# Router, top-2 choice and scatter of a mixture of experts set into local attention's pipeline, and three rounding passes of an FP4 feed-forward set on GpSimd

## Chip, cores and metric

One core of a Trainium2 chip. The metric is device time in microseconds (us) from one launch of the whole program, lower is better. All data are float32.

## What is computed

Four sublayers, one after another, on x of shape (4, 1024, 256). Each adds its output to its input; `_layernorm` has no weights.

```python
x = x + local_attention(_layernorm(x))      # L0_attn: 16 heads, each token sees itself and its two neighbours
x = x + experts(_layernorm(x))              # L0_ffn: 8 experts, top 2
x = x + gated_delta_attention(_layernorm(x))  # L1_attn: a recurrence over 1024 tokens
x = x + fp4_feed_forward(_layernorm(x))     # L1_ffn: 256 -> 704 -> 256

# L0_ffn
logits = x_flat @ router_w + router_b
probs = softmax(logits); top_w, top_idx = top_k(probs, 2)
output = sum over e of comb[:, e] * (gelu(x_flat @ expert_up[e].T) @ expert_down[e].T)

# L1_ffn, before each of its three products
scale = max(|x| in a block of 16) / 6, at least 1e-12
q = nearest of 0, 0.5, 1, 1.5, 2, 3, 4, 6 to |x / scale|, with x's sign, times scale
```

## The kernel before, in words

The program is four blocks in a row, each with its own tiles in memory and its own hand-written instruction streams for the five engines; between blocks all engines meet. Within a block the order on each engine is the order of the calls in its function, and semaphores order the engines against each other. `need(engine, sem, n)` waits until `sem` has reached `n`.

**Local attention** (`local_attention`, L78 to L375). A tile is 128 tokens by 256 features; 32 tiles, taken in 16 pairs, four pairs to a batch row. All engines run through the same steps s = -3 to 17, and in step s each has work on pairs of different age. VectorE: `evict(s)` (queries, keys and values of pair s from PSUM, L230), `scores(s-1)` (L238 to L243), `moments(s+3)` (L203 to L208), `weigh(s-1)` (L248 to L254), `result(s-2)` (L263: projection plus residual). TensorE: `products(s+1, 0)` (L354), `turned_out(s-2)` (L363), `products(s+1, 1)`, `projected(s-2)` (L371), `turned(s+2)` (L343). ScalarE: `turned_out`, `exps`, `normalised(s+3)` (L288) and `turned(s+2)` (L293). GpSimd: `roots(s+3)` (three small instructions, L177 to L179) and `residual(s-1)` (two sums of 256 columns, L184). SyncE loads x, stores results to a stream in device memory, and shifts the keys and values of the edge tiles by one partition for each batch row (L145 to L149), for which `scores` of every fourth pair waits. The first product waits for all loads.

**Mixture of experts** (`mixture_of_experts`, L388 to L787). First the router, over 8 groups of 4 tiles read back from the stream. VectorE: `moments` (L537 to L542), `norm` (normalised rows, L548 and L551), `shift` (bias and maximum of the logits, L555 to L558), `choose` (softmax's sum, the two largest of 8 probabilities, their indices, one-hot counts, L563 to L581), `place` (rank within the expert to row number, L590 to L598). TensorE turns the rows (L704), takes the logits (L713, 16 matmuls) and sums counts (L721, L722). ScalarE copies the turned rows (L660, L665), copies each normalised row for the second expert (L663) and takes the exponentials (L672). GpSimd takes roots (L496) and scatters: for each tile and each of the two choices one indirect DMA of 128 rows into the experts' slots (L491, 64 in all), and at the end 8 more that pad each expert's last tile (L507). ScalarE's DMA queue loads the eight down weights of 1 MB and copies the stream to the accumulator. When the counts are known a table says which expert each of 71 slot tiles belongs to, and where it starts. SyncE waits for all of this and for every scatter, then loads up weights and slot rows tile by tile (L471, L473); TensorE, ScalarE and VectorE work through the 71 tiles, and GpSimd adds the weighted rows into the accumulator (L515).

**Recurrent attention** (`delta_attention`) is not touched by the change.

**FP4 feed-forward** (`fp4_feed_forward`, L1716 on). 32 tiles in 8 trips of 4. `fp4` rounds in nine VectorE passes (L1797 to L1808): block maximum, scale, reciprocal, ratio, exponent bits, a magic number, add it, subtract it, times scale. The hidden rows of each tile (704 columns) are rounded by `round_h`, the normalised rows of a whole trip (1024 columns) at once by `round_z`. VectorE's order per tile n: `result(n-2)` (L1847), `hidden(n)` (two products, L1833), `norm(t+1)` at the second tile of a trip, `round_h(n)`, `round_z(t+1)` behind the third. TensorE: `gate_up(n)` (L1945), `transpose_h(n-1)` (L1955), at the fourth tile `transpose_z(t+1)` (L1934), `down(n-1)` (L1964). GpSimd only takes one root per trip (L1785).

Of the kernel before, what the change touches and what calls it, by code (L numbers as in the profile page):

```python
# [7 lines left out]
ALU = mybir.AluOpType  # L8
# [6 lines left out]
P = 128  # L15
# [62 lines left out]
def local_attention(nc, x_in, consts, w, x_out, B, S, H):  # L78

    DH = D // H
# [4 lines left out]
    scale = DH ** -0.5  # L88
    with ExitStack() as stack:
        m = Scope(nc, stack, "la")  # L90
        ident = m.sb("ident", [P, P]); mhalf = m.sb("mhalf", [P, 1]); neg = m.sb("neg", [P, 2])
        wp = m.sb("wp", [P, KD, D]); wpn = m.sb("wpn", [P, KD, D]); win = m.sb("win", [P, KD, C3]); wc = m.sb("wc", [P, KD, C3]); wo = m.sb("wo", [P, KD, D])
        bp = m.sb("bp", [P, KD]); bpb = m.sb("bpb", [P, KD, P]); braw = m.sb("braw", [P, C3]); bias = m.sb("bias", [P, C3]); bo = m.sb("bo", [P, D])
        x = m.sb("x", [P, 2, TB, D]); z = m.sb("z", [P, 2, 2, D]); zT = m.sb("zT", [P, 2, KD, 2, P])
        st = m.sb("st", [P, 2, 6]); mv = m.sb("mv", [P, 2, 2, 2]); ve = m.sb("ve", [P, 2, 2]); rstd = m.sb("rstd", [P, 2, 2]); nb = m.sb("nb", [P, 2, 2])
        slot = m.sb("slot", [P, 2, TB + 2, C3])
        qk = m.sb("qk", [P, 2, 3, D]); sc = m.sb("sc", [P, 2, 3, H]); mx = m.sb("mx", [P, 2, H]); ex = m.sb("ex", [P, 2, 3, H]); sm = m.sb("sm", [P, 2, H])
        av = m.sb("av", [P, 2, 2, 3, D]); oT = m.sb("oT", [P, 2, KD, 2, P]); xb = m.sb("xb", [P, 2, 2, D]); y = m.sb("y", [P, 2, 2, D])
        ps_qkv = [m.psum(f"ps_qkv{u}", 1024) for u in range(2)]
        ps_z = m.psum("ps_z"); ps_oT = m.psum("ps_oT"); ps_o = [m.psum(f"ps_o{i}") for i in range(2)]  # L100
        loaded = m.sem("loaded"); x_loaded = [m.sem(f"x_loaded{i}") for i in range(4)]; edges = [m.sem(f"edges{i}") for i in range(4)]
        made = m.sem("made"); wpn_psum = m.sem("wpn_psum"); wpn_ready = m.sem("wpn_ready"); wc_psum = m.sem("wc_psum"); wc_ready = m.sem("wc_ready")
# [3 lines left out]
        y_ready = m.sem("y_ready"); stored = [m.sem(f"stored{i}") for i in range(2)]; chain = m.sem("chain"); pool_chain = m.sem("pool_chain")  # L106
        LOADS = 10
        consts["stale"] = m.sems
        in_rows = x_in.rearrange("b (p j) d -> b p j d", j=TB)
        out_rows = x_out.rearrange("(b p j) d -> b p j d", p=P, j=TB)  # L110
        tiles_of = lambda n: [(2 * (n % NP2) + 1 + u) % TB for u in range(2)]
        STEPS = range(-3, NPAIR + 2)
        here = lambda n: 0 <= n < NPAIR
        block = stack.enter_context(nc.Block())
# [6 lines left out]
        def _(sp):  # L121
            def load_x(s):
                b, r = s // NP2, s % NP2
                if s >= 4:
                    need(sp, var_ready, s - 3)
                if s >= 8:
                    need(sp, z_ready, 2 * (s - 7))
                    need(sp, xb_ready, s - 4 if r == 0 else s - 7)
                sp.dma_start(x[:, b % 2, 2 * r:2 * r + 2, :], in_rows[b, :, 2 * r:2 * r + 2, :]).then_inc(x_loaded[s % 4], 16)
# [3 lines left out]
            for dst, src in ((ident[:], consts["ident"]), (mhalf[:], consts["mhalf"]), (wp[:], w["WpT"].rearrange("(k p) n -> p k n", p=P)),  # L133
                             (win[:, :, 0:D], w["WqT"].rearrange("(k p) n -> p k n", p=P)), (win[:, :, D:C3], w["WkvT"].rearrange("(k p) n -> p k n", p=P)),
                             (bp[:], w["bp"]), (braw[:, 0:D], w["bq"].partition_broadcast(P)), (braw[:, D:2 * D], w["bk"].partition_broadcast(P)),
                             (braw[:, 2 * D:C3], w["bv"].partition_broadcast(P)), (bo[:], w["bo"].partition_broadcast(P))):
                sp.dma_start(dst, src).then_inc(loaded, 16)
            sp.dma_start(wo[:], w["WoT"].rearrange("(k p) n -> p k n", p=P)).then_inc(loaded, 16)
# [12 lines left out]
            def store(n):  # L151
                need(sp, y_ready, n + 1)
                for u, j in enumerate(tiles_of(n)):
                    sp.dma_start(out_rows[n // NP2, :, j, :], y[:, n % 2, u, :]).then_inc(stored[n % 2], 16)

            for s in STEPS:
# [4 lines left out]
                if here(s - 3):  # L161
                    store(s - 3)
            store(NPAIR - 1)
            for i in range(2):
                sp.wait_ge(stored[i], 16 * NPAIR)

        @block.gpsimd
        def _(pool):
            pc = Chain(pool, pool_chain)
            pc.link(nc.gpsimd.memset(neg[:], -1.0))  # L170
            pool.wait_ge(loaded, 16 * (LOADS + 1))

            def roots(s):
# [5 lines left out]
                nc.gpsimd.tensor_tensor(nb[:, par, :], nb[:, par, :], neg[:], ALU.mult).then_inc(rstd_ready, 1)  # L179

            def residual(n):
                need(pool, y_ready, n - 1)
                for u, j in enumerate(tiles_of(n)):
                    ins = nc.gpsimd.tensor_tensor(xb[:, n % 2, u, :], x[:, (n // NP2) % 2, j, :], bo[:], ALU.add)  # L184
                ins.then_inc(xb_ready, 1)

            for s in STEPS:
                if here(s + 3):
                    roots(s + 3)
                if here(s - 1):  # L190
                    residual(s - 1)
# [1835 lines left out]
```

## Time and profile before

| | |
|---|---|
| three runs, us | 4022.38, 4025.67, 4015.97 (median 4022.38) |
| the profiled execution, us | 4007.19 |
| its span (first to last instruction), us | 4005.4 |
| mean granted TensorE clock | 0.929 of 2.4 GHz |
| TensorE matmul busy | 3264.1 us, 81% |
| VectorE busy | 2633.9 us, 66% |
| ScalarE busy | 1427.6 us, 36% |
| GpSimd busy | 891.3 us, 22% |

The profile calls the engines PE (TensorE's matmuls), PEld (its weight loads), DVE (VectorE), ACT (ScalarE), POOL (GpSimd) and SP (SyncE); a q behind the name is the engine's DMA queue. L12 is line 12 of the kernel. Tile names begin with their block: la, moe, da, ff. Shares of busy time are means over blocks with different limits, so they are read block by block.

### The profile page before, as it was taken

Reading aid. Unit: us, or ns where it says so; the run is one execution under the profiler, and the core shown is the slowest. Engines: PE = TensorE matmul, PEld = TensorE weight load, DVE = VectorE, ACT = ScalarE, POOL = GpSimd, SP = SyncE. Lnnn points to the kernel's source line nnn. Section 1 sums busy time; section 2 is a strip of 40 time slices with the busy share of each in tenths; the row PEclk is TensorE's granted clock in tenths of the full one; section 3 lists DMA queues with packets and bytes.
Section 4 is the critical chain, followed back from the end, with each engine's and each line's share of the span. In section 5 each row is a group of like instructions: output and inputs, shape, how many; then the busy total and the mean of one; then the engine's idle time right before and its main releaser. Section 6 shows DMA issues by size and latency. Waiting matters only on the chain. (4 is left out here: it accounts for less than half of the span.)

```text
span 4005.4 us, 141798 instructions
## 1 busy us (share of the span) xinstructions
PE 3264.1 (81%) x62854; PEld 2462.9 (61%) x62854; DVE 2633.9 (66%) x5780; ACT 1427.6 (36%) x3252; POOL 891.3 (22%) x1018
## 2 busy tenths in 40 slices
PE   7844999993888888888888888888888888727777
PEld 4633999992566666666655666666566566514555
DVE  6844000002877887887787778877877787667887
ACT  1111212221444454445444444544454444311111
POOL 2316222221223222222322232222223222200000
PEclk9965999996899999999999999999999999858999
DMA  2154666652000000000000000000000000010000
GB/s 63 48 184 143 185 182 179 182 160 89 5 7 11 7 7 11 7 7 7 11 7 7 7 11 7 7 11 7 7 7 11 7 7 5 6 40 14 22 21 14
DMA packets 101423, 172.44 MB, mean 43 GB/s; under 512 B 15128, under 2 KB 75160, under 8 KB 100752
## 3 DMA queue, kind: packets, MB, share of 16 engines
q1 hardware_dynamic: 72592, 127.75, 9.8%
q0 software_dynamic: 19824, 23.03, 4.0%
q10 hardware_dynamic: 8400, 12.58, 0.9%
q8 instruction: 501, 8.21, 0.9%
q14 instruction: 106, 0.87, 0.1%
HBM read 125.35 MB, written 40.05 MB: 41 GB/s over the span
## 5 line engine op out<-in xcount | busy, mean ns | idle before, releaser
L962 POOL TENSOR_TENSOR da_M<-da_M,da_decay 128x512 f32<-128x512 f32 x256 | 279.9, 1122 | 634.8 <-DVE da_M L1125 323.1
L1268 ACT COPY da_Ub<-da_U 32x256 f32<-32x256 f32 x1024 | 412.0, 402 | 17.4
L1102 DVE TENSOR_TENSOR da_eGn<-da_eGn,da_z 128x30 f32<-128x30 f32 (+14 forms) x960 | 352.6, 367 | 33.0
L643 DVE TENSOR_SCALAR moe_y<-moe_ps_dn,moe_zs 128x256 f32<-128x256 f32 x71 | 34.4, 484 | 510.1 <-PE moe_ps_dn L769 510.1
L1101 DVE TENSOR_TENSOR da_z<-da_eGn 128x30 f32<-128x30 f32 (+14 forms) x960 | 348.7, 363 | 27.6
L1554 PE MATMUL da_C<-da_Ub,da_Km 128*64 128x256 f32 x2048 | 302.8, 417 | 23.3 <-ACT da_Ub L1268 9.5
L759 PEld LDWEIGHTS moe_ps_up<-moe_zsT,moe_up 128*128 128x128 f32 x2272 | 266.2, 193 | 5.4 <-ACT moe_zsT L676 1.8
L759 PE MATMUL moe_ps_up<-moe_zsT,moe_up 128*128 128x128 f32 x2272 | 266.9, 276 | 1.2 <-ACT moe_zsT L676 1.2
L1386 PE MATMUL da_unit<-da_wx,da_xnT 128*128 128x512 f32 x512 | 257.8, 628 | 3.7 <-DVE da_sp L1045 2.7
L769 PE MATMUL moe_ps_dn<-moe_down,moe_hT 128*128 x1136 | 256.8, 379 | 0.0
L1393 PE MATMUL da_unit<-da_xnT,da_wx 128*128 128x128 f32 x2048 | 245.5, 279 | 12.4 <-ACT da_eGn L1253 12.4
L1393 PEld LDWEIGHTS da_unit<-da_xnT,da_wx 128*128 128x128 f32 x2048 | 236.8, 194 | 19.9 <-ACT da_eGn L1253 19.9
L1125 DVE TENSOR_TENSOR da_M<-da_C,da_M 128x512 f32<-128x512 f32 x256 | 176.0, 687 | 98.7 <-PE da_C L1554 96.3
L1261 ACT COPY da_U<-da_A 128x256 f32<-128x256 f32 x256 | 95.5, 373 | 379.7 <-PE da_A L1525 378.9
L682 ACT ACTIVATE moe_hT<-moe_ps_up 128x512 f32<-128x512 f32 x142 | 84.8, 597 | 406.2 <-PE moe_ps_up L759 406.2
L769 PEld LDWEIGHTS moe_ps_dn<-moe_down,moe_hT 128*128 128x128 f32 x1136 | 210.5, 190 | 25.6
L1525 PE MATMUL da_A<-da_W,da_TT 32*32 32x64 f32 x8192 | 180.0, 224 | 51.7 <-DVE da_W L1112 30.4
L955 POOL TENSOR_TENSOR da_v<-da_v,da_norm 128x256 f32<-128x256 f32 x128 | 116.7, 1205 | 448.7 <-ACT da_v L1240 448.7
L1554 PEld LDWEIGHTS da_C<-da_Ub,da_Km 128*64 128x64 f32 x2048 | 137.8, 143 | 115.2 <-issue 59.4
L1541 PE MATMUL da_B<-da_U,da_gm 32*32 32x64 f32 x8192 | 171.5, 219 | 42.3 <-ACT da_U L1261 24.5
L1525 PEld LDWEIGHTS da_A<-da_W,da_TT 32*32 32x32 f32 x8192 | 133.9, 109 | 114.1 <-issue 47.9
L515 POOL DMA_INDIRECT moe_acc<-moe_y,moe_zs x71 | 110.0, 1549 | 419.9 <-DVE moe_y L643 417.0
(289 smaller groups left out, 6830.4 us busy)
## 6 DMA issues: line engine op xcount, KB each, us to landing
moe_up<-in_upT SPq DMA_DIRECT2D x71, 1024.0 KB, 5.1
moe_zs<-moe_slots SPq DMA_DIRECT2D x71, 129.0 KB, 4.2
moe_down<-in_downT ACTq DMA_DIRECT2D x8, 1024.0 KB, 12.0
la_x<-in_x SPq DMA_DIRECT2D x16, 256.0 KB, 3.9
stream<-la_y SPq DMA_DIRECT2D x32, 128.0 KB, 2.3
moe_x<-stream SPq DMA_DIRECT2D x8, 512.0 KB, 4.9
da_x<-moe_acc SPq DMA_DIRECT2D x128, 32.0 KB, 2.0
stream<-da_xz SPq DMA_DIRECT2D x128, 32.0 KB, 1.8
```

The source lines that it names most:

```text
L759: ins = nc.tensor.matmul(ps_up[j][:, f * P:(f + 1) * P], up[:, n % UB, k, (j * HB + f) * P:(j * HB + f + 1) * P], zsT[:, n % 2, k, :], sta ...
L769: ins = nc.tensor.matmul(ps_dn[n % 2][:, 0:D], hT[:, n % 2, f, :], down[:, bass.ds(expert[n] + f * D, D)], start=(f == 0), stop=(f == FB - 1))
L962: ins = nc.gpsimd.tensor_tensor(st_, st_, decay[:, par, rec, 2 * g:2 * g + 2].rearrange("p a b -> p (a b)").unsqueeze(2).to_broadcast([P, ...
L1101: c.link(tt(t, Xm[:, s + 1:C, s:s + 1].to_broadcast([P, below, s]), Xm[:, s:s + 1, 0:s].to_broadcast([P, below, s]), ALU.mult))
L1102: c.link(tt(Xm[:, s + 1:C, 0:s], Xm[:, s + 1:C, 0:s], t, ALU.add))
L1125: tt(st_, Cp[:], st_, ALU.add).then_inc((s_updated, r_updated)[rec], 1)
L1268: ins = nc.scalar.copy(Ub[rows_of(b), :, :, b, :], U[rows_of(b), rec])
L1386: ins = mm(bank, xnT[:, par, kk, :], wx[:, kk, u // 2, cols], start=(kk == 0), stop=(kk == KD - 1))
L1393: ins = mm(bank[:, hp * P:(hp + 1) * P], wx[:, kk, j, col:col + P], xnT[:, par, kk, :], start=(kk == 0), stop=(kk == KD - 1))
L1525: ins = mm(wu[rw, q_, 2 + rec, j], TT[rw, of_solve(g, q_, rec, j), :], W[rw, rec, q_, j], start=True, stop=True)
L1541: ins = mm(po[rw, q_, 1, j], gm[rw, par, g, q_, (first + j) * C:(first + 1 + j) * C], U[rw, rec, q_, j], start=False, stop=(rec == 1), ski ...
L1554: ins = mm(Cp[feat(q_), j * B * DH:(j + 1) * B * DH], Km[:, g, rec, j, DH * q_:DH * (q_ + 1)], Ub[:, q_, j].rearrange("p b e -> p (b e)"), ...
```

## The change

`local_attention` now only notes its inputs, and `mixture_of_experts` holds attention, router and experts as one block. The steps run to 22, and `part_of(s, lag)` says which group of four tiles (two pairs), if any, has its router part in step s. A group's moments stand in odd steps, its normalised rows, turned rows, logits and shift in the even step after, exponentials in the next, choice at a lag of 6, places at 7, scatter at 8. Tokens are numbered by attention's own tiles, and results stay in memory for the router while they are stored straight into the accumulator; the read back and the copy are gone. Normalised rows for both choices are made by ScalarE. The residual is added into x's own tile, which has three batch rows of room. Weighted values and projections have one buffer, not two. Down weights lie where the key and value rows were, and are loaded by SyncE behind `av_ready` of the last pair. Padding rows are written by ScalarE's DMA queue at addresses read into a register.

```diff
+            for s in STEPS:
+                if part_of(s, 8) is not None:
+                    scatter(part_of(s, 8))
+                if here(s - 1):
+                    residual(s - 1)
+                if here(s + 3):
+                    roots(s + 3)
+                if part_of(s, 3) is not None:
+                    roots2(part_of(s, 3))
...
+            for s in STEPS:
+                if here(s):
+                    evict(s)
+                if here(s - 1):
+                    scores(s - 1)
+                if s >= 0 and here(s + 3):
+                    moments(s + 3)
+                if part_of(s, 6) is not None:
+                    choose(part_of(s, 6))
+                if here(s - 1):
+                    weigh(s - 1)
+                if here(s - 2):
+                    result(s - 2)
+                if part_of(s, 7) is not None:
+                    place(part_of(s, 7))
+                if part_of(s, 3) is not None:
+                    moments2(part_of(s, 3))
+                if part_of(s, 4) is not None:
+                    shift(part_of(s, 4))
...
+            def router_rows(g, r):
+                b = g % 2
+                need(act, rstd2_ready, g + 1)
+                need(act, scattered[g % XB], (g // XB) * 16 * 2 * ST)
                 for s in range(ST):
+                    nc.scalar.activation(zx[:, g % XB, s, r, 0:D], y[:, b, s, :], ACT.Identity, bias=nb2[:, b, s:s + 1], scale=rstd2[:, b, s:s + 1]).then_inc(z2_ready, 1)
...
+            for s in STEPS:
+                if part_of(s, 4) is not None:
+                    router_rows(part_of(s, 4), 0)
+                if here(s - 2):
+                    turned_out(s - 2)
+                if part_of(s, 5) is not None:
+                    exps2(part_of(s, 5))
+                if here(s - 1):
+                    exps(s - 1)
+                if part_of(s, 4) is not None:
+                    turned_rows(part_of(s, 4), 0)
+                if here(s + 3):
+                    normalised(s + 3)
+                if part_of(s, 4) is not None:
+                    turned_rows(part_of(s, 4), 1)
+                if here(s + 2):
+                    turned(s + 2)
+                if part_of(s, 4) is not None:
+                    router_rows(part_of(s, 4), 1)
...
+            act.wait_ge(pad_ready, 1)
+            for e in range(E):
+                at = act.value_load(padidx[0:1, e:e + 1], min_val=0, max_val=DUMP)
+                act.dma_start(slots[bass.ds(at, P), :], pad[:]).then_inc(padded, 16)
...
+            for s in STEPS:
+                if part_of(s, 7) is not None:
+                    ranks(part_of(s, 7))
+                if here(s + 1):
+                    products(s + 1, 0)
+                if here(s - 2):
+                    turned_out(s - 2)
+                if part_of(s, 4) is not None:
+                    turned_rows(part_of(s, 4), 0)
+                if here(s + 1):
+                    products(s + 1, 1)
+                if here(s - 2):
+                    projected(s - 2)
+                if part_of(s, 4) is not None:
+                    turned_rows(part_of(s, 4), 1)
+                if here(s + 2):
+                    turned(s + 2)
+                if part_of(s, 4) is not None:
+                    logits(part_of(s, 4))
...
+            sp.wait_ge(av_ready, NPAIR)
+            for e in range(E - 1):
+                load_down(e)
             store(NPAIR - 1)
+            load_down(E - 1)
```

In the feed-forward, `round_z` ends on VectorE with the magic number; `norm(t+1)` moves to the first tile of a trip and `round_z(t+1)` behind the second.

```diff
             for t in range(TRIPS):
                 pool.wait_ge(var_ready, t + 1)
                 nc.gpsimd.tensor_tensor(rstd[:], ve[:], mhalf[:].to_broadcast([P, UN]), ALU.pow).then_inc(rstd_ready, 1)
+                pool.wait_ge(z_scaled, t + 1)
+                pc.link(nc.gpsimd.tensor_tensor(zlevel[:], zratio[:], zmagic[:], ALU.add))
+                pc.link(nc.gpsimd.tensor_tensor(zlevel[:], zlevel[:], zmagic[:], ALU.subtract))
+                if t > 0:
+                    pool.wait_ge(zT_psum, t * 2)
+                nc.gpsimd.tensor_tensor(blocks(qz[:].rearrange("p u d -> p (u d)")), blocks(zlevel[:]),
+                                        zscl[:].unsqueeze(2).to_broadcast([P, WIDE // FP4_BLOCK, FP4_BLOCK]), ALU.mult).then_inc(qz_ready, 1)
...
-                if u == 1 and t + 1 < TRIPS:
+                if u == 0 and t + 1 < TRIPS:
                     norm(t + 1)
                 round_h(n)
-                if u == 2 and t + 1 < TRIPS:
+                if u == 1 and t + 1 < TRIPS:
                     round_z(t + 1)
```

## Rows read from the trace of the kernel before

**Rows 1.** Busy us by stretch: PE, PEld, DVE, ACT, POOL; PEclk, DMA share, GB/s

```profile
0.00:239.40 239.40, 183.13 (x860) 134.74 (x860) 173.18 (x326) 40.48 (x81) 57.08 (x85) 0.96 0.17 52
...
239.40:389.10 149.70, 55.24 (x232) 47.63 (x232) 68.59 (x406) 20.16 (x56) 79.17 (x86) 0.50 0.57 188
...
3605.00:4005.40 400.40, 310.79 (x1152) 208.52 (x1152) 318.87 (x539) 69.28 (x177) 7.05 (x7) 0.89 0.06 18
```

**Rows 2.** Timeline, an attention pair: start, us, engine, line, operation, [idle before, releaser]

```profile
62.39 0.69 DVE L263 TENSOR_TENSOR la_y<-la_ps_o,la_xb 128x512 f32<-128x512 f32 x1
...
63.00 1.81 DVE L230 TENSOR_TENSOR la_slot<-la_ps_qkv,la_bias 128x768 f32<-128x768 f32 x2
...
73.93 0.69 DVE L263 TENSOR_TENSOR la_y<-la_ps_o,la_xb 128x512 f32<-128x512 f32 x1 [0.55 <-PE la_ps_o L371]
```

**Rows 3.** Timeline from the last attention result to the first expert transpose

```profile
235.85 0.69 DVE L263 TENSOR_TENSOR la_y<-la_ps_o,la_xb 128x512 f32<-128x512 f32 x1 [7.65 <-PE la_ps_o L371]
...
378.63 0.96 POOL L507 DMA_INDIRECT moe_slots<-moe_pad,moe_padidx  x1 [0.30 <-issue]
379.89 0.96 POOL L507 DMA_INDIRECT moe_slots<-moe_pad,moe_padidx  x1 [0.30 <-issue]
...
389.15 0.69 PE L749 MATMUL moe_ps_t<-moe_ident,moe_zs 128*128 128x128 f32 x2 [26.36 <-DMA moe_zs<-moe_slots]
```

**Rows 4.** Timeline of one group in the router

```profile
308.82 0.18 DVE L563 TENSOR_REDUCE moe_sm<-moe_pexp 128x4 f32<-128x32 f32 x1
...
312.41 1.41 DVE L537 BATCH_NORM_STATS2 moe_st<-moe_x 128x6 f32<-128x256 f32 x4
...
313.30 3.56 PE L713 MATMUL moe_ps_l<-moe_rw,moe_zT 128*128 128x8 f32 x16
...
314.35 0.18 DVE L590 TENSOR_TENSOR moe_rank<-moe_ps_dn,moe_base 128x32 f32<-128x32 f32 x1
...
315.15 0.17 DVE L598 CAST moe_idx<-moe_pos 128x8 uint32<-128x8 f32 x1
```

**Rows 5.** Timeline of GpSimd and ScalarE in an attention pair

```profile
70.43 0.75 POOL L177 TENSOR_TENSOR la_rstd<-la_ve,la_mhalf 128x2 f32<-128x2 f32 x1 [10.58 <-DVE la_ve L208]
...
72.53 2.16 POOL L184 TENSOR_TENSOR la_xb<-la_x,la_bo 128x256 f32<-128x256 f32 x2
...
72.61 1.09 ACT L288 ACTIVATE la_z<-la_x,la_nb,la_rstd 128x256 f32<-128x256 f32 x2 [2.21 <-POOL la_nb L179]
...
74.37 0.59 ACT L293 COPY la_zT<-la_ps_z 128x512 f32<-128x512 f32 x1 [0.67 <-PE la_ps_z L343]
```

**Rows 6.** Busy time by stretch, columns as in rows 1, attention's end

```profile
216.00:218.00 2.00, 2.00 (x11) 2.00 (x11) 0.00 (x0) 0.00 (x0) 0.34 (x1) 0.50 0.34 112
```

**Rows 7.** Timeline of the feed-forward: a trip of four tiles

```profile
3702.15 0.42 DVE L1847 TENSOR_TENSOR ff_y<-ff_ps_y,ff_x 128x256 f32<-128x256 f32 x1
...
3724.51 0.52 DVE L1833 TENSOR_TENSOR ff_h<-ff_silu,ff_ps_u 128x352 f32<-128x352 f32 x1 [1.78 <-ACT ff_silu L1892]
...
3747.21 1.23 DVE L1806 TENSOR_TENSOR ff_level<-ff_ratio,ff_magic 128x1024 f32<-128x1024 f32 x1
...
3750.87 0.42 DVE L1847 TENSOR_TENSOR ff_y<-ff_ps_y,ff_x 128x256 f32<-128x256 f32 x1
```

**Rows 8.** GpSimd's groups by line: operation, shapes, count, busy us, mean ns, idle

```profile
L962 POOL TENSOR_TENSOR da_M<-da_M,da_decay 128x512 f32<-128x512 f32 x256 | 279.9, 1122 | 634.8 <-DVE da_M L1125 323.1
...
L515 POOL DMA_INDIRECT moe_acc<-moe_y,moe_zs x71 | 110.0, 1549 | 419.9 <-DVE moe_y L643 417.0 <-DMA moe_acc<-moe_y,moe_zs 2.9
...
L947 POOL TENSOR_TENSOR da_xz<-da_x,da_z 128x256 f32<-128x256 f32 x32 | 23.2, 726 | 312.8 <-DVE da_z L1031 312.8
```

**Rows 9.** Timeline of GpSimd and VectorE in the recurrent attention

```profile
1099.36 1.36 POOL L955 TENSOR_TENSOR da_v<-da_v,da_norm 128x256 f32<-128x256 f32 x2 [14.04 <-ACT da_v L1240]
...
1099.55 0.69 DVE L1102 TENSOR_TENSOR da_eGn<-da_eGn,da_z 128x234 f32<-128x234 f32 x1
...
1101.00 0.40 DVE L1102 TENSOR_TENSOR da_eGn<-da_eGn,da_z 128x228 f32<-128x228 f32 x1
```

More of the change, by code:

```diff
@@ L160, in _ @@
                     shift_edges(s // NP2)
-                if here(s - 3):
+                if here(s - 3) and s - 3 < NPAIR - 1:
                     store(s - 3)
+            sp.wait_ge(av_ready, NPAIR)
+            for e in range(E - 1):
+                load_down(e)
             store(NPAIR - 1)
-            for i in range(2):
-                sp.wait_ge(stored[i], 16 * NPAIR)
+            load_down(E - 1)
+            sp.wait_ge(where_ready, 1)
+            sp.wait_ge(cleared, 32)
+            sp.wait_ge(padded, 16 * E)
+            for b in range(XB):
+                sp.wait_ge(scattered[b], 16 * 2 * ST * ((GROUPS - b + XB - 1) // XB))
+            for n in range(SLOT_TILES):
+                if n >= ZB:
+                    sp.wait_ge(added[(n - ZB) % 2], 16 * ((n - ZB) // 2 + 1))
+                if n >= UB:
+                    sp.wait_ge(up_psum, 2 * (n - UB) + 2)
+                which = sp.value_load(where[0:1, 2, n:n + 1], min_val=0, max_val=(E - 1) * KD)
+                sp.dma_start(up[:, n % UB], up_rows[:, bass.ds(which, KD), :]).then_inc(up_loaded[n % UB], 16)
+                row = sp.value_load(where[0:1, 1, n:n + 1], min_val=0, max_val=DUMP)
+                sp.dma_start(zs[:, n % ZB, :], slots[bass.ds(row, P), :]).then_inc(zs_loaded[n % ZB], 16)
         @block.gpsimd
@@ L187, in _, with scatter @@
+            def scatter(g):
+                b = g % XB
+                need(pool, idx_ready, g + 1)
+                need(pool, z2_ready, 2 * ST * (g + 1))
+                for s in range(ST):
+                    for r in range(2):
+                        nc.gpsimd.indirect_dma_start(slots[:], bass.IndirectOffsetOnAxis(ap=idx[:, b, r, s:s + 1], axis=0),
+                                                     zx[:, b, s, r, :], None).then_inc(scattered[b], 16)
             for s in STEPS:
+                if part_of(s, 8) is not None:
+                    scatter(part_of(s, 8))
+                if here(s - 1):
+                    residual(s - 1)
@@ L193, in _ @@
+            for b in range(2):
+                pool.wait_ge(added[b], 16 * ((SLOT_TILES - b + 1) // 2))
         @block.vector
@@ new lines, in place @@
+            def place(g):
+                need(dve, rank_psum, g + 1)
+                c.link(tt(rank[:], ps_k.rearrange("p (s e) -> p s e", e=E), base[:].unsqueeze(1).to_broadcast([P, ST, E]), ALU.add))
+                for r in range(2):
+                    ins = tt(prod[:, r], hot[:, r], rank[:], ALU.mult)
+                c.link(ins)
+                c.link(nc.vector.tensor_reduce(pos[:], prod[:], AX, ALU.add))
+                need(dve, scattered[g % XB], (g // XB) * 16 * 2 * ST)
+                nc.vector.tensor_copy(idx[:, g % XB], pos[:]).then_inc(idx_ready, 1)
@@ L281, in _ @@
+            for n in range(SLOT_TILES):
+                dve.wait_ge(zs_loaded[n % ZB], 16 * (n // ZB + 1))
+                weigh(n)
         @block.scalar
@@ L305, in _, with turned_rows, exps2 @@
+            def turned_rows(g, half):
+                need(act, zT2_psum, 2 * g + half + 1)
+                need(act, logit_psum, g)
+                nc.scalar.copy(zT2[:, :, 2 * half:2 * half + 2, :], ps_r[:].rearrange("p (k u t) -> p k u t", k=KD, u=2)).then_inc(zT2_ready, 1)
+            def exps2(g):
+                need(act, shifted, g + 1)
+                need(act, hot_ready, g)
+                nc.scalar.activation(pe_[:], lm[:], ACT.Exp).then_inc(exp2_ready, 1)
             for s in STEPS:
+                if part_of(s, 4) is not None:
+                    router_rows(part_of(s, 4), 0)
@@ L731, in _ @@
+                if part_of(s, 4) is not None:
+                    logits(part_of(s, 4))
+            need(pe, idx_ready, GROUPS)
+            mm(ps_cnt, ones[:], before[:, (GROUPS - 1) % 2, ST, :], start=True, stop=True).then_inc(count_psum, 1)
             pe.wait_ge(table_ready, 1)
             for i in range(3):
[L733 removed]
+                ins = mm(ps_tab[:, i * P:(i + 1) * P], table[:, i:i + 1], ident[:], start=True, stop=True)
```

648 lines of the change are left out of this document (276 added, 372 removed).

## Prediction

> **What bounds the kernel now.** I first cut the run into its four blocks with the table by stretch [rows 1]: local attention to 239.4 us, the router with its scatter to 389.1, then the experts and the recurrent attention, which the change leaves as they are, and the feed-forward's loop over tiles from 3605. In the router's 149.7 us no engine is full (TensorE 55, VectorE 69, GpSimd 79) and TensorE has a granted clock of 0.50, its level of 1.2 GHz: that block is bound by latency and by GpSimd's queue. In attention the clock is 0.96.
>
> Next the timeline of one attention pair. The result of a pair starts every 11.54 us [rows 2], and VectorE waits 0.55 us for the projection: a loop of eviction, TensorE's products, turning, products and projection (63.00 to 73.93, 10.9) and the result (0.6), with VectorE only half a microsecond from being the bound itself. So work added to VectorE lengthens the step almost in full.
>
> Then the joins [rows 3]: the last attention result starts at 235.85, the last GpSimd write of the router at 379.89, the first expert transpose at 389.15. The writes, 72 of them, end 1.26 us apart: GpSimd's queue is what the router waits for at its end.
>
> **Change, part 1: the router inside attention.** I follow the time of the last scatter write, since the experts wait for it as before and cost the same afterwards (71 slot tiles, same loads, same instructions).
>
> Removed: all between the last result and the last write, 379.89 - 235.85 = 144.0 us: block change, reload of rows, the queue of expert weights, eight groups, eight padding writes. The padding writes go to ScalarE's DMA queue, eight pairs of register load and issue, which no row shows there; at GpSimd's 1.26 each they take 10 us. They begin once the count is known, while GpSimd still writes the last group: costed at nothing, up to 5 us if that cover is gone. The expert weights now follow on SyncE's queue after the last weighted values, 8 MB. In the router stage 188 GB/s moved on average [rows 1], which makes 43 us: they would land some 2 us before the last write. I cost that at nothing, and 5 us if they are late; SyncE itself is not needed before.
>
> Start: three more small loads ahead of the first product, 0.5 us of issue each, +2.
>
> Attention steps. Per group of four tiles VectorE gains [rows 4]: choice 3.6 (308.82 to 312.41), moments 1.9 (to 314.35), placing 1.0 (to the end of the cast at 315.15), the shift of logits 0.6 (three passes of 0.2, like the one at 308.82), token numbers 0.2 and 0.3 for results written as two tiles. Sum 7.6. Normalised rows leave VectorE for ScalarE, which is 17% busy in attention [rows 1]. In steps 3 to 6, where nothing is scattered yet, that is the whole price: two groups, +15.
>
> From step 8 on each even step also has a scatter on GpSimd, in its queue ahead of the residual and of the next pair's roots. VectorE's step ends with the shift, which needs the logits, whose last copy stands on ScalarE behind the normalising of the next pair, which needs these roots. So the chain from one group's moments to the next is: roots 2.1, eight writes 10.1, residual 2.2, roots 2.1 [rows 3, 5], normalising 1.1, copy 0.6, logits (16 matmuls, 3.56 at half clock [rows 4], 1.8 at full: I take 2.7 since TensorE has just idled), shift 0.6, eviction to the end of the projection 10.9 [rows 2], result 0.8, placing 1.0, moments 1.9. Sum 36.1, with 12 handovers of about 0.1, 37. Two steps were 23.1. Three such cycles (steps 8 to 13): +42. VectorE's own need, 2 x 11.0 + 7.6 = 29.6, is below it: it idles some 5 us in each even step.
>
> Steps 14 to 17 have no more roots; choice, moments and placing stay: +15. The wait of one pair in four for shifted edge rows (a step of 12.6 in place of 11.54, three times) is covered by the longer steps: -3.
>
> Sum up to the last result: 2 + 15 + 42 + 15 - 3 = +71.
>
> Tail: result 0.8, moments 1.9, roots 2.1, then the scatters of the last three groups, 3 x 10.1 less the last write's own 1.3. The middle one waits some 2 us for its places. That is 36 against 144.0: -108.
>
> Net of part 1: **-37**. Bounds: if TensorE's clock never falls, logits take 1.8 and no product is stretched: about -53. If every logit and transpose of the router runs at half clock and what follows it too: about -20. The rows speak for between: near attention's end, behind a gap in TensorE's work, the clock was 0.50 with TensorE busy throughout [rows 6], and each new cycle has two gaps of about 5 us (one while VectorE places and takes moments, one before the logits).
>
> **Change, part 2: three rounding passes on GpSimd.** A trip of four tiles takes 48.72 us (3702.15 to 3750.87 [rows 7]). Its two additions and the scaling of 1024 columns take VectorE 3.66 (3747.21 to 3750.87). Seven trips lose them; the first one, with nothing beside it, gets GpSimd's time instead.
>
> GpSimd's price: no row has 1024 columns. Above: four times the 256-column sum, 4 x 0.73 = 2.9; below: twice the 512-column product, 2 x 1.12 = 2.2 [rows 8]. I take 2.3, nearest by width, 2.0 for the product with a broadcast scale: 6.8 with handovers. TensorE asks for the rows one tile later, over 10 us on, so this is hidden, up to passes of about 3.7.
>
> But it costs VectorE: where GpSimd multiplied from 1099.36 on, a VectorE product took 0.69, and not the 0.40 of one six columns narrower at 1101.00 [rows 9]; it waited for GpSimd. After its part VectorE has 2.3 us of passes that read PSUM or one operand (result, two products, maxima), which cover GpSimd's first pass; then its two-operand scaling waits out the second (1.9) and the next pass the third (1.9). That takes back the 3.66. What is left comes from slack: an ordinary tile has a wait of 1.78 for TensorE [rows 7], and a stall there costs nothing. Of 3.8 stalled I count 2.3 as swallowed, so 2.2 to 2.5 gained per trip: 7 x 2.4 = 17, less 3 in the first trip: **-14**. Bounds: no blocking, 7 x 4 - 3 = -25; passes of 2.9 with nothing swallowed, +5.
> The Trainium skill (SBUF — State Buffer, Who interferes with whom) says that a VectorE instruction with two SBUF inputs and a GpSimd instruction that reads SBUF exclude each other for the whole instruction. By that rule the blocking is full, as I count it; without it part 2 would be -25. The trace agrees in the 0.29 us added at 1099.55.
>
> **Sum.** -37 - 14 = -51. The profiled execution took 4007.2 us (span 4005.4); it lies 15 us below the median of the three runs, 4022.4. Against itself the change makes 3956, against the median **3971 us**. I call anything within 0.3% (12 us) no change, about what a measurement of this kernel can tell.
>
> **Rivals.**
> (a) The clock holds and GpSimd's passes slip between: attention's clock was 1.00 at steady load; against it, the gaps of 5 us. Gain 53 + 25 = 78: 3944. Chance 0.16.
> (b) The port eats the feed-forward's gain: GpSimd's passes near 2.9, no slack left; for it the 256-column row. Gain 37 - 0 to 5: 3988. Chance 0.14.
> (c) Scatter instructions get longer beside attention's VectorE work, as the adding ones of the expert stage, 1.55 us and not 0.96 [rows 8]. They bound the cycle: 8 x 0.6 = 4.7 for three cycles and 14 for the tail, +28: 3999. Against it: in the router stage they kept 1.26 with VectorE at 69 us of 150. Chance 0.06.
> The Trainium skill (SBUF — State Buffer, SBUF: two separate sides) has a rule for it: VectorE in a two-port mode keeps GpSimd from writing descriptors. By it the copies of the choice would be the culprits.
> (d) Slower: TensorE drops to 1.2 GHz and stays there through the joined steps. Then its part of about 9.9 in the 10.9 is 19.8 in each step: cycles of 50 for 37 (+39), steps 3 to 6 about 25 for 15.6 (+38), the last ones +25, sum +102, so 4073. It decides for slower once over six tenths of the steps run so. For it: clock 0.50 all through the router [rows 1]; against: busy 55 of 150 there, here about two thirds, and 0.89 in the feed-forward loop at 78% busy. Chance 0.08.
> (e) Little happens: hidden waits (late expert weights, padding, edge rows behind stores on SyncE) take 40 us. Chance 0.06.
> Forecast 0.50.
>
> **Numbers.** Faster: forecast, a, b, c, 0.86; same: e, 0.06; slower: d, 0.08. The range runs from just below (a) to just above (c) and leaves out d, most of e and the edges: 3936 to 4006.
>
> **What would show it.** First expert transpose at about 352 (389.15 - 37). Attention results about 15.5 apart at first, then pairs of 37 with idle time of VectorE ahead of the shift, released by the logits, and GpSimd's scatter ahead of the roots. Granted clock dipping, not lying, at 0.50. Feed-forward trips of about 46.3 for 48.7; VectorE's two-operand passes of the third tile stretched by up to 2; GpSimd passes of 2.0 to 2.9. Wrong: scatter spacing over 1.3, expert loads after the last write, trips over 48.

## The result, and the profile after

| | median, us | ratio to the kernel before, 95% interval |
|---|---|---|
| changed kernel | 3961.66 (4 runs, 3951.86 to 3966.98) | 0.9856 [0.9838, 0.9875] |
| kernel before, beside it | 4019.18 (4 runs) | |
| changed kernel once more, another chip | 3949.42 (5 runs) | 0.9853 [0.9831, 0.9875] |
| kernel before, beside it | 4007.66 (10 runs) | |

By the medians the change is worth 58 us, 1.45%; the forecast was 51. Two pairs of profiles say where. The second pair comes from one chip. Stages end at the first expert transpose, at the first clearing pass of the recurrent attention, and at the first weight transpose of the feed-forward.

| us | router's end | experts | recurrence | feed-forward | span |
|---|---|---|---|---|---|
| before, first profile | 389.1 | 529.4 | 2621.0 | 465.8 | 4005.4 |
| after, first profile | 360.1 | 530.5 | 2627.3 | 446.3 | 3964.3 |
| before, same chip | 391.0 | 529.1 | 2613.5 | 466.1 | 3999.7 |
| after, same chip | 353.9 | 530.4 | 2620.8 | 445.6 | 3950.7 |
| difference, first profiles | -29.0 | +1.1 | +6.3 | -19.5 | -41.1 |
| difference, same chip | -37.1 | +1.3 | +7.3 | -20.5 | -49.0 |

The recurrence is the same code in all of them. It took 2613 to 2627 us in the profiles of this study, in kernels with and without the change, so its +7.3 is not put down to the change; nor is it explained. A profile is one execution: on the one chip that of the kernel before ran 6 us below its kernel's median and that of the changed kernel 3 above, which is why the medians show 58 us and this pair 49.

Busy time by stretch in the changed kernel's first profile, columns as in rows 1, answering to [rows 1]: attention with the router, the tail, the feed-forward's loop.

```profile
0.00:308.04 308.04, 234.09 (x1052) 169.40 (x1052) 221.56 (x611) 76.20 (x158) 101.11 (x153) 0.87 0.22 66
308.04:360.11 52.07, 9.91 (x40) 7.86 (x41) 16.26 (x105) 5.44 (x11) 24.67 (x27) 0.54 0.70 232
...
3582.00:3964.00 382.00, 309.26 (x1152) 206.15 (x1152) 315.31 (x517) 68.62 (x177) 62.34 (x31) 0.92 0.06 18
```

The joins, from the second profile, answering to [rows 3]: last attention result, padding issues of ScalarE's queue, table of tiles, last write, first weight load, first expert transpose.

```profile
309.16 0.76 DVE L405 TENSOR_TENSOR le_y<-le_ps_o,le_x 128x256 f32<-128x256 f32 x2 [8.48 <-PE le_ps_o L665]
...
333.88 8.68 ACTq L599 DMA_DIRECT2D moe_slots<-le_pad  x8
...
337.68 0.55 DVE L513 CAST le_where<-le_ps_r 1x384 uint32<-1x384 f32 x1 [1.53 <-PE le_ps_r L718]
...
344.95 0.96 POOL L301 DMA_INDIRECT moe_slots<-le_zx,le_idx  x1 [0.30 <-issue]
...
348.52 0.41 SPq L255 DMA_DIRECT2D le_up<-in_upT  x1
...
353.92 0.69 PE L734 MATMUL le_ps_z<-le_ident,le_scr 128*128 128x128 f32 x2 [16.27 <-DMA le_scr<-moe_slots]
```

Attention became 72 us longer (last result at 235.85 before, at 308.04 and 309.16 after), and the tail from there to the transpose went from 153.3 us to 52.1 in the first profile and 44.8 here. Here padding ends before the last write begins, and SyncE begins 3.6 us after that write's start (3.8 in the kernel before): the last write is what the experts wait for. In the first profile they wait for the padding (see the experiments).

One cycle of two steps, GpSimd, ScalarE, TensorE and VectorE, second profile:

```profile
180.26 1.81 DVE L371 TENSOR_TENSOR le_down<-le_ps_qkv,le_bias 128x768 f32<-128x768 f32 x2
...
182.51 1.47 POOL L301 DMA_INDIRECT moe_slots<-le_zx,le_idx  x1 [0.53 <-issue]
...
191.87 0.96 POOL L301 DMA_INDIRECT moe_slots<-le_zx,le_idx  x1 [0.30 <-issue]
192.85 2.89 POOL L284 TENSOR_TENSOR le_x<-le_x,le_bo 128x256 f32<-128x256 f32 x2
195.72 0.72 POOL L277 TENSOR_TENSOR le_rstd<-le_ve,le_mhalf 128x2 f32<-128x2 f32 x1
...
197.02 1.09 ACT L532 ACTIVATE le_scr<-le_x,le_nb,le_rstd 128x256 f32<-128x256 f32 x2 [6.53 <-POOL le_nb L279]
...
198.63 2.57 PE L684 MATMUL le_ps_r<-le_rw,le_zT 128*128 128x8 f32 x16 [3.80 <-ACT le_zT L559]
...
201.24 0.19 DVE L422 TENSOR_TENSOR le_lg<-le_ps_r,le_rb 128x32 f32<-128x32 f32 x1 [5.40 <-PE le_ps_r L684]
```

This is the forecast chain, link by link: eight writes ahead of residual and roots, ScalarE idle 6.53 for the roots, TensorE 3.80 for the copy, VectorE 5.40 for the logits. The cycle is 37.8 us (180.26 to 218.05), and the other two are alike: VectorE waits 5.19 and 5.61 for the logits there.

In the first profile the cycles are as long, 37.5, 37.4 and 35.4 us, but the waits are others. The shift of the first cycle, and the logits of the second:

```profile
161.89 0.19 DVE L422 TENSOR_TENSOR le_lg<-le_ps_r,le_rb 128x32 f32<-128x32 f32 x1 [2.16 <-PE le_ps_r L684]
```

```profile
197.19 1.95 PE L684 MATMUL le_ps_r<-le_rw,le_zT 128*128 128x8 f32 x16 [0.24 <-ACT le_zT L559]
```

VectorE waits 2.16, 0.73 and no visible time ahead of the three shifts, and 2.5 to 3.4 us for attention's exponentials instead, since ScalarE saw TensorE's turned values late (last section). So the forecast chain sets the cycle in one of the two profiles; that the other has the same length is chance.

A feed-forward trip of the first profile, answering to [rows 7]: the result, GpSimd's passes, and the two VectorE passes beside them.

```profile
3711.66 0.42 DVE L1851 TENSOR_TENSOR ff_y<-ff_ps_y,ff_x 128x256 f32<-128x256 f32 x1
...
3714.59 2.63 DVE L1796 SCALAR_TENSOR_TENSOR ff_ratio<-ff_h,ff_inv 128x704 f32<-128x704 f32 x1
3717.26 2.14 DVE L1798 TENSOR_SCALAR ff_expo<-ff_ratio 128x704 uint32<-128x704 uint32 x1
```

```profile
3711.70 2.35 POOL L1775 TENSOR_TENSOR ff_zlevel<-ff_zratio,ff_zmagic 128x1024 f32<-128x1024 f32 x1 [19.06 <-DVE ff_zmagic L1831]
3714.13 2.35 POOL L1776 TENSOR_TENSOR ff_zlevel<-ff_zlevel,ff_zmagic 128x1024 f32<-128x1024 f32 x1
3716.55 2.46 POOL L1779 TENSOR_TENSOR ff_qz<-ff_zlevel,ff_zscl 128x1024 f32<-128x1024 f32 x1
```

The scaling (0.89 alone) ends only behind GpSimd's second pass (3716.48), the exponent pass (0.53 alone) only behind the third (3719.01): 1.74 and 1.61 us lost, 3.35 per trip. The block maximum and reciprocal ahead of them keep their length.

### The profile page after: what moved, and what is told of

The parts are those of the page before. It is cut to its first block and busy times, and to the rows that moved or that the text cites. A ratio compares the mean times of both kernels' runs of the same rounds, so it can differ in the third digit from the quotient of the medians.

```text
span 3964.3 us, 141871 instructions
## 1 busy us (share of the span) xinstructions
PE 3280.4 (83%) x62854; PEld 2462.8 (62%) x62854; DVE 2626.6 (66%) x5740; ACT 1448.3 (37%) x3284; POOL 940.0 (24%) x1051
## 5 line engine op out<-in xcount | busy, mean ns | idle before, releaser
L744 PEld LDWEIGHTS le_ps_qkv<-le_scr,le_up 128*128 128x128 f32 x2272 | 267.3, 193 | 5.4 <-ACT le_scr L588 1.8
L744 PE MATMUL le_ps_qkv<-le_scr,le_up 128*128 128x128 f32 x2272 | 267.9, 277 | 1.2 <-ACT le_scr L588 1.2
L1378 PE MATMUL da_unit<-da_xnT,da_wx 128*128 128x128 f32 x2048 | 244.7, 278 | 10.6 <-ACT da_eGn L1238 10.5
L594 ACT ACTIVATE le_scr<-le_ps_qkv 128x512 f32<-128x512 f32 x142 | 84.8, 597 | 407.3 <-PE le_ps_qkv L744 375.1
L321 POOL DMA_INDIRECT moe_acc<-le_scr x71 | 110.8, 1561 | 427.1 <-DVE le_scr L519 424.1
L519 DVE TENSOR_SCALAR le_scr<-le_ps_oT,le_scr 128x256 f32<-128x256 f32 x36 | 17.4, 484 | 260.5 <-PE le_ps_oT L754 260.5
L1526 PEld LDWEIGHTS da_B<-da_U,da_gm 32*32 32x32 f32 x8192 | 134.0, 107 | 82.4 <-issue 45.7
L1204 ACT ACTIVATE da_sp<-da_sp 128x512 f32<-128x512 f32 x128 | 79.6, 630 | 276.5 <-DVE da_sp L1030 275.7
```

Source lines behind the costliest of these rows:

```text
L744: ins = nc.tensor.matmul(ps_up[j][:, f * P:(f + 1) * P], up[:, n % UB, k, (j * HB + f) * P:(j * HB + f + 1) * P], zsT[:, n % 2, k, :], sta ...
L1378: ins = mm(bank[:, hp * P:(hp + 1) * P], wx[:, kk, j, col:col + P], xnT[:, par, kk, :], start=(kk == 0), stop=(kk == KD - 1))
L1526: ins = mm(po[rw, q_, 1, j], gm[rw, par, g, q_, (first + j) * C:(first + 1 + j) * C], U[rw, rec, q_, j], start=False, stop=(rec == 1), ski ...
```

## Experiments

### The two parts, each alone

The first takes the feed-forward of the kernel before; the second takes attention, experts and router of the kernel before, and the feed-forward of the changed one. No line within a part differs.

> Part 1 alone: attention, router and experts as in the changed kernel, the feed-forward as before. Theory: the two parts are independent, so this takes part 1's share: first expert transpose at 360.1 (389.15 before), that is -29 us, or -0.7%; feed-forward trips stay at 48.7. Rival: the parts share something (a shifted clock, the state in which the recurrence starts), and the shares don't add up: then this is -45 or more of the 57 us of the medians, or under -20.

> Part 2 alone: the feed-forward of the changed kernel behind attention, router and experts as before. Theory: trips of 45.2 to 46.8 for 48.7, first trip 3 us later, in all -20 us (-0.5%), first expert transpose at 389. Rival: the port takes it back once the blocks before are as they were: trips over 48, below -5 us.

Part 1 alone: 0.9906 [0.9892, 0.9921], first expert transpose at 359.2, feed-forward stage 465.1. Part 2 alone: 0.9963 [0.9949, 0.9978], feed-forward stage 444.6. The shares add up (0.94% and 0.37% against 1.45%) within their intervals. In the second one's profile the router stage, unchanged, ended at 397.7, 7 to 9 us later than in the two profiles of the kernel before. By stages part 2 is worth 20 to 21 us, where the ratio gives 15 and the difference of the medians 18.

### The feed-forward: order alone, passes alone

Order alone, on the kernel before:

```diff
-                if u == 1 and t + 1 < TRIPS:
+                if u == 0 and t + 1 < TRIPS:
                     norm(t + 1)
                 round_h(n)
-                if u == 2 and t + 1 < TRIPS:
+                if u == 1 and t + 1 < TRIPS:
                     round_z(t + 1)
```

Passes alone: the three passes on GpSimd, with these two conditions as before.

> The kernel before with only the order of the feed-forward's work moved: norm behind the first tile of a trip, rounding behind the second, all nine passes on VectorE. Theory: VectorE's work per trip is unchanged and its 5.9 us of waits for TensorE stay, so trips stay within 0.5 us of 48.7. Rival: the earlier rounding itself removes waits (of the 5.9 us, 2.9 are left in the changed kernel): trips of 46 to 47.

> The kernel before with only the three passes on GpSimd, and norm and rounding behind the second and third tile as before. The order alone shortened the feed-forward stage by 10 us (465.8 to 455.6), both together by 20 (446.3). Theory A: the two are additive, so this gives about 10: stage 455, trips near 47.3. Theory B: the passes gain only by the slack that the order puts behind them; here VectorE's stalls of 3.4 us per trip eat the 3.7 us that it saves: stage 463 to 466, trips 48.3 or more.

Order alone: 0.9955 [0.9941, 0.9969], stage 455.6, so -10. Passes alone: **slower**, 1.0065 [1.0044, 1.0085], stage 495.5, so +30. Both: -20. Neither of my two theories had the loss. Its place, in the kernel with the passes alone:

```profile
3756.51 2.46 POOL L1794 TENSOR_TENSOR ff_qz<-ff_zlevel,ff_zscl 128x1024 f32<-128x1024 f32 x1
```

```profile
3747.54 0.82 PE L1974 MATMUL ff_ps_h<-ff_ident,ff_qh 128*128 128x128 f32 x6
3759.02 1.11 PE L1953 MATMUL ff_ps_z<-ff_ident,ff_qz 128*128 128x128 f32 x4 [10.67 <-POOL ff_qz L1794]
...
3761.78 3.62 PE L1983 MATMUL ff_ps_y<-ff_downT,ff_hqT 128*128 128x256 f32 x8
```

TensorE turns the rounded rows at the fourth tile, ahead of `down`. With rounding behind the third tile it now idles 10.7 us for GpSimd's last pass, and VectorE then waits 3.3 to 4.5 for the result: trips of 52 to 53 us. Rounding a tile earlier puts that time beside `down` and the gate and up products of the next tile. In the kernel with the order alone, two trips:

```profile
3694.76 0.42 DVE L1847 TENSOR_TENSOR ff_y<-ff_ps_y,ff_x 128x256 f32<-128x256 f32 x1
3695.90 0.52 DVE L1833 TENSOR_TENSOR ff_h<-ff_silu,ff_ps_u 128x352 f32<-128x352 f32 x1 [0.72 <-ACT ff_silu L1892]
...
3742.76 0.42 DVE L1847 TENSOR_TENSOR ff_y<-ff_ps_y,ff_x 128x256 f32<-128x256 f32 x1
3743.79 0.52 DVE L1833 TENSOR_TENSOR ff_h<-ff_silu,ff_ps_u 128x352 f32<-128x352 f32 x1 [0.62 <-ACT ff_silu L1892]
```

48.0 us apart, 47.9 on the mean of four, against 48.75 on the mean of five in the kernel before on one of these chips. From the second result of the stage to the 26th, six trips, it is 287.0 us for 293.3: 6 of the 10 us. Of the rest 3.3 lie ahead of the second result and 0.7 behind the 26th. VectorE's waits in the six fell from 6.1 to 5.1 us a trip. I had expected trips within 0.5 us of 48.7, so this too was a small miss. Passes on top of the order: 45.2 to 47.0 a trip, 276.2 and 276.7 us for the six.

### GpSimd's queue

```diff
             for s in STEPS:
-                if part_of(s, 8) is not None:
-                    scatter(part_of(s, 8))
                 if here(s - 1):
                     residual(s - 1)
                 if here(s + 3):
                     roots(s + 3)
                 if part_of(s, 3) is not None:
                     roots2(part_of(s, 3))
+                if part_of(s, 8) is not None:
+                    scatter(part_of(s, 8))
```

> The changed kernel with one step of GpSimd moved: the scatter of a group stands behind the residual and the roots of its step, not ahead of them. Theory (GpSimd's queue sets the cycle): roots come at about 188 and not 193.5 in a cycle that begins at 179.5, so the four cycles of 35 to 37.5 fall to VectorE's own need of 30 to 32: last attention result some 20 us earlier than 308.0, time -0.5% against the changed kernel. Rival: what holds the cycle is TensorE's late semaphore updates (turned values done at 188.7, seen by ScalarE at 193.4), which a scatter brings wherever it stands: then the cycles stay over 34 and the result comes at most 8 us earlier.

0.9852 [0.9838, 0.9866], not to be told from the change. Roots come at 180.4 in a cycle from 172.0, but the last result only at 303.8, 4 us earlier; the cycle from 172.0 is still 36.3. So in this profile GpSimd's queue alone is not the bound. Two others may be. One is the rival as written: the result came under 8 us earlier, and in the second and third cycle (36.3 and 37.7 us) VectorE sees TensorE's results late. In the first cycle nothing is seen late, and it takes 32.1. The other shows in the cycle's second half.

### TensorE's clock

Granted clock in an odd step of the changed kernel's first profile (0.50 is 1.2 GHz, 1.00 is 2.4): the first tile's products, in two stretches, and the rest of the step.

```profile
200.83:203.50 2.67, 2.67 (x4) 1.15 (x5) 2.60 (x4) 0.00 (x0) 0.00 (x0) 0.50 0.02 3
203.50:206.10 2.60, 2.60 (x7) 1.70 (x6) 2.50 (x5) 0.00 (x0) 0.00 (x0) 0.50 0.06 17
206.10:216.80 10.70, 7.69 (x45) 6.13 (x43) 6.99 (x27) 2.45 (x6) 1.10 (x3) 0.98 0.21 71
```

From 76 us on all eleven steps that have products begin like this: the first tile's in 4.3 to 5.5 us, where the second tile's take 2.75 and the first tile's took 2.82 before. TensorE had idled ahead of them: up to 4.2 us ahead of an even step, while VectorE took moments, and 2.4 and 0.8 us within the 7 us ahead of the odd step shown, for the copy of the turned values and for the shift. So I gave it work in the gap, whose result nothing reads:

```diff
                 if part_of(s, 4) is not None:
                     logits(part_of(s, 4))
+                if here(s - 2):
+                    for i in range(4 if s % 2 else 1):
+                        mm(ps_oT[:], ident[:], wc[:, 0, 0:512], start=True, stop=True)
```

> The changed kernel with idle matmuls (128 rows by 512 columns, result never read) at the end of each attention step: four in odd steps, one in even ones, in a PSUM bank that is free there. Theory: each step begins at a granted clock of 0.50, because TensorE has just idled 3.4 to 4.2 us while VectorE takes moments; its first four products take 4.5 to 5.5 us for 2.8. With the gap filled they take 2.8, each step shortens by 1.7 to 2.6, and the last attention result comes 20 to 30 us earlier than 308.0; time -0.5 to -0.7% against the changed kernel. Rival: the fillers only delay the first products and the dips stay, or VectorE is the bound anyway: the result within 5 us of 308.

> The same fillers together with the scatter behind the roots. Theory: both act on the same cycle in different places, so the result comes another 4 us (what the moved scatter gave alone) to 15 us earlier (with the products fast again, GpSimd's ten microseconds are what is left in an even step) than with the fillers alone. Rival: late semaphore updates of TensorE beside a scatter take it back: within 3 us of the fillers alone.

> Scatter behind the roots and more fillers: five in odd steps and three in even ones, for four and one. Theory: odd steps still begin at 0.50 (first products 4.2 to 5.5 us) because TensorE idles while it waits for the copy and for ranks; three fillers cover that, so cycles fall from 32 or 33 to about 31 (VectorE's need), last result some 5 us earlier than 292. Rival: the fillers at the end of an even step stand in front of products that VectorE already waits for: result later than 292.

Fillers alone: 0.9845 [0.9827, 0.9864], last result at 308.8. The even steps' products are back at 2.82 (odd steps still begin in 3.5 to 5.5), and nothing is gained: the cycle from 178.2 is 39.7. VectorE now waits 6.4 us for the logits in each of the three cycles: with the fillers the forecast chain through GpSimd holds the cycle. Fillers with the scatter behind the roots: 0.9789 [0.9770, 0.9808], last result at **292.1**, 16 us earlier; cycles of 32 to 33. More fillers: result at 281.3, where I had expected some 5 us less than 292, and cycles of 30.6 to 30.8, but the same time, 0.9788 [0.9763, 0.9813]. TensorE and VectorE in a cycle of the kernel with both:

```profile
208.85 2.82 PE L648 MATMUL le_ps_qkv<-le_scr 128*128 128x512 f32 x8 [0.76 <-DVE le_down L371]
```

```profile
174.60:207.74 33.14, 31.11 (x143) 21.79 (x142) 28.86 (x86) 9.98 (x21) 15.50 (x21) 0.90 0.21 68
207.74:239.68 31.94, 29.91 (x143) 20.98 (x142) 27.77 (x81) 9.00 (x19) 14.37 (x18) 0.95 0.15 51
```

Where the fillers alone give nothing and the scatter moved on top of them 16.7 us, two profiles of one chip and both without late updates, GpSimd's queue was the limit that held. That the clock is a second one of its own shows in the step to more fillers: with every first product at 2.8, the result comes another 11 us earlier (another chip, also without late updates). What is left is near VectorE's need of 29.6. These two last kernels beat both the kernel before and the change. What is not shown is that the few fillers are needed for the 16 us. The scatter moved alone was profiled, and timed, only on a chip where TensorE's updates came late (last section), and its one cycle without them took 32.1 us, as with both changes (32.0). Its runs were no faster than the change; whether the clock or the late updates held them, a run on a chip without late updates would tell, and there is none.

### The padding

```diff
+            sp.wait_ge(pad_ready, 1)
+            for e in range(E // 2):
+                at = sp.value_load(padidx[0:1, e:e + 1], min_val=0, max_val=DUMP)
+                sp.dma_start(slots[bass.ds(at, P), :], pad[:]).then_inc(padded, 16)
             sp.wait_ge(where_ready, 1)
...
-            for e in range(E):
+            for e in range(E // 2, E):
                 at = act.value_load(padidx[0:1, e:e + 1], min_val=0, max_val=DUMP)
```

The other experiment puts the eight writes back on GpSimd, as indirect DMAs behind the last scatter.

> The changed kernel with four of the eight padding writes on SyncE's queue, which is idle then, the other four on ScalarE's. Theory: the padding queue (8 x 2.09 us, SyncE let go at 353.5) ends the wait before the experts, with the table of tiles (348.6) next: the first expert transpose comes at about 355 for 360.1, -5 us. Rival 1: padding was not last, the transpose stays at 360. Rival 2: the table's chain is late because of these very issues (its steps have waits of 0.6 to 3.9 us that the kernel before does not show), then it gets earlier too and the transpose comes at 350 to 352.

> The changed kernel with the eight padding writes back on GpSimd's queue, behind the last scatter. If the padding queue on ScalarE had been hidden, as the forecast has it, this costs 10 us: first expert transpose at 370. Theory now: the padding on ScalarE hid little, so it costs 3 to 5 us: writes end at 355, SyncE let go at 358, transpose at 363 to 365. And if the issues on ScalarE's queue are what slows the table's chain beside the scatter (13 us from the counts on, 3.9 before), that chain is short here, its table ready at 340 or before.

The first profile of the changed kernel had misled me: padding took 16.69 us there and ended last. Split: 0.9849 [0.9835, 0.9863], transpose at 358.5 for the 355 expected; the four issues left on ScalarE took 14.3 us, nearly what eight had, and SyncE's four 14.1 beside them. So the number of issues on a queue did not set it. On GpSimd: 0.9870 [0.9847, 0.9893], transpose at 369.1. Its last result came at 313.8, 4.6 later than in the change's second profile; the other 10.6 of the 15.2 us are the eight writes. So in an undisturbed profile ScalarE's queue hides them whole, as forecast. The table's chain was short there, 3.8 us from the counts, but so it is in the second profile with the issues on ScalarE, so they are not what slows it.

### The same two kernels again

No edit.

> The changed kernel once more, beside the kernel before on the same chip. If the profiled execution of the first measurement was a plain one, the first expert transpose comes at 358 to 362, the feed-forward stage takes 446 us, and the ratio lies at 0.985 to 0.988. If its recurrence (2627 us, against 2613 to 2617 in all kernels profiled since) was out of the ordinary, it is 2615 here.

> The kernel before, profiled on this chip. The router stage ended at 389.2, 391.3 and 397.7 in three profiles of kernels that share it. If that is the chip's scatter from run to run, it ends anywhere between 389 and 398 here; the recurrence takes 2613 to 2617 as in the others, 2621 in the first profile.

Padding took 8.68 us, the table was ready at 337.7 (348.1 in the first profile), the transpose came at 353.9: 4 us earlier than I had expected. The recurrence was 2620.8 and 2613.5, so neither it nor 2627 is out of the ordinary by itself.

## Why the prediction was right, and where it was not

- **The whole.** Forecast -51; measured -58 by the medians, -49 by the pair of profiles from one chip, -41 by the first pair. Right in sign and size. The parts were forecast at -37 and -14. Part 1 is -37.1 in one pair and -29.0 in the other, part 2 -20.5 and -19.5. In the first pair the parts sum to -48.5, near the forecast by chance: a tail 7 us longer is set off by what part 2 gave beyond its forecast.
- **Start and attention steps, +71.** Measured +72: +20.2 up to the eviction of step 8 for 17, +38.9 in the three scatter cycles for 39 (42 - 3), +13.1 behind them for 15. The excess ahead of the cycles fits the clock, which the forecast had for the logits alone: with more fillers, where every first product takes 2.8, step 8 begins 4.4 us earlier. The chain behind the 42 is in the trace of the second profile only ("some 5" are 5.2 to 5.6 there). And it is not the only bound of that length: with the scatter out of it the result came 4 us earlier and not 20, if in a profile with late updates.
- **Tail, 36.** Measured 35.9 (308.04 to 343.98), and 35.8 in the second profile. First expert transpose forecast for 352: 353.9 and 360.1.
- **Padding costed at nothing, up to 5 us without cover.** 8.68 us in one profile, hidden; 16.69 in the other, where the tail is 52.1 us for 44.8. That is 7 us, two more than my bound.
- **Expert weights on SyncE.** Traffic in the tail was 274 GB/s in the second profile, not the 188 I took, and nothing waited for them.
- **Part 2, -14: measured -20, the trips as forecast.** GpSimd's passes took 2.35, 2.35 and 2.46 for 2.3, 2.3 and 2.0; the blocking 3.35 per trip for 3.8; the late first trip 3.06 for 3. "Of 3.8 stalled I count 2.3 as swallowed" held over six trips, from the stage's second result to its 26th: VectorE's waits (it waits for ScalarE's `silu`, and that for TensorE) fell from 6.1 to 3.7 or 3.8 us a trip. The trips last 46.0 to 46.1 us there, where 46.3 was forecast, and 48.9 before: 17 us for the six.
- **Part 2, the missing 6 us.** The term that was mis-sized is "less 3 in the first trip": the three are lost ahead of the first gate product, but outside the six trips the stage is still 3 us shorter (169.4 to 169.7 us for 172.6 to 172.8), where one more trip less 3 makes a loss of 0.6. And I credited the gain to the passes. Half of the 20 us comes from the moved order, which I used only as cover and priced at nothing: it takes 10 us alone, 3.3 of them ahead of the second result; without that order the passes cost 30. "TensorE asks for the rows one tile later, so this is hidden" held; the price had that cover been gone was never worked out. The bound without blocking counts 4 us a trip where the rows give 3.66, so it should read -23, not -25.
- **Rivals.** (b) The port eats the gain: VectorE loses 3.35 of the 3.66 us that it was freed of, yet the waits behind give 2.3 back. The Trainium skill (SBUF — State Buffer, Who interferes with whom) says that a VectorE instruction with two SBUF inputs and a GpSimd instruction that reads SBUF contend under an exclusive lock, and that copies, casts and passes with a constant can contend too. The trace agrees with both: 2.63 for 0.89 in the scaling, 2.14 for 0.53 in the exponent pass. (c) Longer scatter writes: spacing stayed 1.27; the first of a group took 1.47 and two others 1.7. (d) Clock at 0.50 throughout: it dipped and came back, 0.87 on the mean. (e) Hidden waits: 7 us in one profile. (a) Clock holds: it did not; fillers alone gain nothing, and once the scatter stands behind the roots, keeping the clock up in odd steps too is worth 11 us up to the last result.

## What to carry to other kernels

When work leaves an engine, try the new order without the move and the move without the new order: here the order gives 10 us, the move alone costs 30, and both together give 20. Compare a loop over several trips and over its ends, not over one trip: here trips alternate between 45.2 and 47.0 us. When a loop's chain passes through several engines and one is relieved without effect, look for a second limit of about the same length, a clock that dips at each start or results that are seen late among them, before writing the idea off, and repeat the profile on another chip. Read the last join in more than one profile: in one the padding was the last to arrive, in another it was hidden.

## What the hardware showed beyond that

In some profiles, while scatters run, an engine sees another's result late. In the change's first profile TensorE's turned values were done at 188.7, and ScalarE, with nothing else to do, went on at 193.45:

```profile
185.81 2.86 PE L657 MATMUL le_ps_oT<-le_ident,le_scr 128*128 128x128 f32 x24
```

```profile
193.45 0.59 ACT L547 COPY le_down<-le_ps_oT 128x512 f32<-128x512 f32 x1 [10.14 <-remote]
```

In the second profile the same wait ended at once, 189.25 for 189.2. In the first, the padding issues (16.69 us for eight) and the table's chain on VectorE (13 us from the counts on, 3.9 in the kernel before) were slow as well:

```profile
334.76 16.69 ACTq L599 DMA_DIRECT2D moe_slots<-le_pad  x8
...
344.42 0.15 DVE L509 TENSOR_SCALAR le_first<-le_first 128x1 f32<-128x1 f32 x1 [3.86 <-remote]
```

It went with the chip or the run, not with the kernel: the changed kernel has it in one profile and not in the other. Three kernels profiled on one chip have it (18.4 and 17.8 us for eight issues, 14.3 for four); on two other chips, five profiles with the router inside attention don't. It costs the tail some 7 us (52.1 for 44.8), and the cycles are no longer with it than without (37.4 and 37.8), though the waits in them differ. What holds the updates up stays open, and so does whether it happens in executions that are not profiled.

The kernel with more fillers reaches its first expert transpose 10.6 us earlier than the one with few (326.2 for 336.8) and is no faster by the medians. In its profile 6 us of that are gone by the end, in blocks whose code is the same (the recurrence 3.2 of them); that is within what these blocks vary by from one profile to the next, and why the medians show nothing at all stays open.
